# A two-layer graph network on one core: the tensor engine's semaphore increments moved from the last product of a group to a drain behind it

## The reference

```python
def gnn0(x, edge_attr, src, dst):          # 4 heads of 32
    m = x @ W_n2m.T
    q, k, v = m @ Wq.T + bq, m @ Wk.T + bk, m @ Wv.T + bv
    e = edge_attr @ W_edge.T @ We.T        # one row of 128 for each edge
    alpha = sum_c(q[dst] * (k[src] + e)) / sqrt(32)
    alpha = softmax over the edges of one dst
    out = segment_sum((v[src] + e) * alpha, dst)
    x_r = m @ Wskip.T + bskip
    beta = sigmoid([out, x_r, out - x_r] @ Wbeta.T)
    return (beta * x_r + (1 - beta) * out) @ W_m2n.T

def gnn1(x, src, dst, w):                  # one head of 256
    scores = sum(q[dst] * k[src]) / 16 + w * we + be
    attn = softmax over the edges of one dst
    out = segment_sum(v[src] * attn, dst)
    x = layer_norm(x + out + x @ ws + bs)
    return layer_norm(x + gelu(x @ w_ff1 + b1) @ w_ff2 + b2)

x = layernorm(x + gnn0(x, ...)); x = layernorm(x + gnn1(x, ...))
```

## Time and profile before

| | us |
|---|---|
| median of the timed runs | 5051.74 |
| profiled execution, first to last instruction (span) | 6753.4 |
| first node phase | 0 to 107 |
| edge phase of the first layer | 107 to 3131 |
| second node phase | 3131 to 3407 |
| edge phase of the second layer | 3407 to 6401 |
| last node phase | 6401 to 6753.4 |
| TensorE busy / VectorE busy | 4299.6 / 3831.3 |
| ScalarE busy / GpSimd busy | 3003.4 / 3308.1 |
| mean granted TensorE clock | 0.79 |

### The profile page before, as it was taken

One profiled execution on the slowest core, in us unless ns is written; L12 is line 12 of the kernel. 1 busy time (PEld: TensorE's weight loads), 2 busy tenths in 40 slices (PEclk: granted clock), 3 DMA queues, 4 the chain that ended last, 5 costly groups with the idle time before them and its releaser, 6 DMA issues.

```text
span 6753.4 us, 105844 instructions
## 1 busy us (share of the span) xinstructions
PE 4299.6 (64%) x23291; PEld 3492.8 (52%) x23291; DVE 3831.3 (57%) x12902; ACT 3003.4 (44%) x6997; POOL 3308.1 (49%) x3637
## 2 busy tenths in 40 slices
PE   6555555565565566566746666666666666666698
PEld 3454554555455555454534555555554555554587
DVE  4565665666566666666734444455454444444588
ACT  1444454555454454554324444444444444444432
POOL 2545555455555455452355545554555554454355
PEclk8777777777777777777978778787888787777899
DMA  6555555555555555553446556565666665555422
GB/s 201 148 145 148 146 145 146 145 153 148 149 152 145 145 152 154 148 148 99 122 141 163 161 153 162 157 162 157 164 160 158 160 160 158 157 163 158 125 73 70
DMA packets 774181, 996.11 MB, mean 147 GB/s; under 512 B 189569, under 2 KB 559489, under 8 KB 773553
## 3 DMA queue, kind: packets, MB, share of 16 engines
q10 hardware_dynamic: 394272, 443.81, 23.8%
q0 software_dynamic: 150224, 410.39, 22.7%
q1 hardware_dynamic: 229056, 135.14, 7.5%
HBM read 862.98 MB, written 125.90 MB: 146 GB/s over the span
## 4 chain that ended last, share of the span: by engine, by line
another core or an unknown queue 22%; PE 21%; DVE 17%; issue 16%; DVEq 7%; ACTq 5%; ACT 5%; DMA 2%; POOL 2%; SPq 1%; POOLq 1%
PE ps L1377 20%; DVE rows L1009 2%; DVE score L1021 2%; DVE prod L1033 2%; ACT oh L750 2%; DVE acc L1174 2%; DMA acc_d<-acc 2%; ACT place L738 1%; ACTq L827 1%; DVE prod L1016 1%; DVEq L1233 1%; ACTq L730 1%; SPq L266 1%; DVEq L1231 1%
## 5 line engine op out<-in xcount | busy, mean ns | idle before, releaser
L637 POOL DMA_INDIRECT rows<-kv_d,src_all x1564 | 1535.2, 982 | 1543.1 <-DVE score L1021 951.0
L637 POOL DMA_INDIRECT rows<-x_d,src_all x1564 | 1487.0, 951 | 1450.5 <-DVE prod L1033 962.3
L1377 PE MATMUL ps<-place 128*128 128x256 bf16 (+2 forms) x10560 | 1459.9, 288 | 296.4 <-issue 186.8
L1377 PEld LDWEIGHTS ps<-place 128*128 128x128 bf16 (+1 forms) x10560 | 1250.9, 149 | 587.4 <-issue 317.6
L1377 PE MATMUL ps<-rows,oh 128*128 x3520 | 1093.2, 470 | 457.3 <-DVE oh L1154 340.7
L1033 DVE SCALAR_TENSOR_TENSOR prod<-rows,ps 128x256 f32<-128x256 f32 x1760 | 637.3, 418 | 906.8 <-remote 549.9
L1377 PEld LDWEIGHTS ps<-rows,oh 128*128 128x128 f32 x3520 | 797.8, 236 | 617.9 <-issue 478.8
L750 ACT ACTIVATE oh<-iota_row,rel 128x128 f32<-128x128 f32 x2640 | 837.9, 388 | 552.9 <-remote 408.8
L1377 PE MATMUL ps<-msg,oh 128*128 128x132 f32 x3520 | 607.0, 330 | 595.8 <-DVE msg L1149 331.8
L1377 PEld LDWEIGHTS ps<-msg,oh 128*128 128x128 f32 x3520 | 544.1, 235 | 638.9 <-DVE msg L1149 421.0
L738 ACT ACTIVATE place<-dst_row,node_tab 128x512 f32<-128x512 int32 (+1 forms) x880 | 613.2, 708 | 385.4 <-DVE acc L1174 145.3
(11 more groups left out here) (217 smaller groups left out, 4152.9 us busy)
## 6 DMA issues: line engine op xcount, KB each, us to landing
dst_row<-in_dst_row ACTq DMA_DIRECT2D x880, 256.0 KB
place<-q_d ACTq DMA_DIRECT2D x440, 192.8 KB
acc_d<-acc ACTq DMA_DIRECT2D x440, 128.5 KB
ea<-in_ea SPq DMA_DIRECT2D x440, 128.0 KB
acc_d<-acc ACTq DMA_DIRECT2D x440, 66.0 KB
place<-q_d ACTq DMA_DIRECT2D x440, 64.0 KB
rows<-kv_d,src_all POOLq DMA_INDIRECT x1564
rows<-x_d,src_all POOLq DMA_INDIRECT x1564
```

The source lines that it names most:

```text
L637: pool.indirect_dma_start(out=L.rows[:, t % SLOTS, j, 0:D], out_offset=None, in_=L.table, in_offset=bass.IndirectOffsetOnAxis(ap=src_all[: ...
L1377: return pe.matmul(out_, lhsT=lhsT, rhs=rhs, start=first, stop=last)
```

## The change

In both edge phases, each of the ten increments of TensorE moves off the product it stood on: the product has none, and behind it stands `pe.drain()` with the increment. Products, waits, their order, and all other engines are as before. The node phases keep their increments on the products. The drains are 440 each behind edge_keys, queries and back in the first layer, 440 each behind queries (with its bias products) and back in the second, and five for each of 55 chunks in both: 1595 and 1155, in all 2750.

```diff
@@ -1424,8 +1424,8 @@
                         after(pe, s["added"], g - 1)
                         pe.wait_ge(s["ld_ea"][st % PLACES], loads_done(L, c, st))
                         for j in range(JT // 2):
-                            i = mm(e_ps(b)[:, 2 * j * DM:2 * (j + 1) * DM], ea[st % PLACES][:, j * P:(j + 1) * P], w_c[:, :])
-                        i.then_inc(s["e"], 1)
+                            mm(e_ps(b)[:, 2 * j * DM:2 * (j + 1) * DM], ea[st % PLACES][:, j * P:(j + 1) * P], w_c[:, :])
+                        pe.drain().then_inc(s["e"], 1)
 
                 def queries_ready(c, st):
                     pe.wait_ge(s["ld_q"][st % PLACES], loads_done(L, c, st))
@@ -1439,46 +1439,49 @@
                     for j in range(JT):
                         parts = 1 if L is L0 else 3
                         for m in range(parts):
-                            i = mm(q_ps(L, b)[:, j * L.D:(j + 1) * L.D], L.oht[st % PLACES][:, j * P:(j + 1) * P],
+                            mm(q_ps(L, b)[:, j * L.D:(j + 1) * L.D], L.oht[st % PLACES][:, j * P:(j + 1) * P],
                                    L.qw[st % PLACES][:, m * (D + 1):m * (D + 1) + L.D], m == 0, m == parts - 1)
                     if L is L0 or st == 1:
-                        i.then_inc(s["q"], 1)
+                        pe.drain().then_inc(s["q"], 1)
 
                 def bias_products(par, st):
 
                     if L is L1:
                         for j in range(JT):
                             n = st * JT + j
-                            i = mm(qb_ps[par][:, 3 * n:3 * (n + 1)], L.oht[st % PLACES][:, j * P:(j + 1) * P],
+                            mm(qb_ps[par][:, 3 * n:3 * (n + 1)], L.oht[st % PLACES][:, j * P:(j + 1) * P],
                                    L.qw[st % PLACES][:, D::D + 1])
                         if st != 1:
-                            i.then_inc(s["q"], 1)
+                            pe.drain().then_inc(s["q"], 1)
 
                 def turn(c):
                     stand_by(pe, gate, s["masked"], c + 1)
                     sc = biased[:, :, 0:H].rearrange("p n h -> p (n h)") if H == HEADS else biased[:, :, 0]
                     pn = pen[:, :, 0:H].rearrange("p n h -> p (n h)") if H == HEADS else pen[:, :, 0]
                     pe.transpose(turn_ps[0:R, 0:P], sc, ident[:, :])
-                    pe.transpose(turn_ps[0:R, P:2 * P], pn, ident[:, :]).then_inc(s["turned"], 1)
+                    pe.transpose(turn_ps[0:R, P:2 * P], pn, ident[:, :])
+                    pe.drain().then_inc(s["turned"], 1)
 
                 def arrange(c):
                     stand_by(pe, gate, s["ends"], c + 1)
-                    mm(arr_ps[0:H, :], sel_h[H][0:R, :], spread[0:R, :, :].rearrange("p m n -> p (m n)"))\
-                        .then_inc(s["arranged"], 1)
+                    mm(arr_ps[0:H, :], sel_h[H][0:R, :], spread[0:R, :, :].rearrange("p m n -> p (m n)"))
+                    pe.drain().then_inc(s["arranged"], 1)
 
                 def carry_back(c):
                     stand_by(pe, gate, s["carries"], c + 1)
-                    mm(back_ps[0:R, :], sel_ht[H][0:H, 0:R], carry[0:H, :, :].rearrange("p m n -> p (m n)"))\
-                        .then_inc(s["spreadback"], 1)
+                    mm(back_ps[0:R, :], sel_ht[H][0:H, 0:R], carry[0:H, :, :].rearrange("p m n -> p (m n)"))
+                    pe.drain().then_inc(s["spreadback"], 1)
 
                 def turn_back(c):
                     stand_by(pe, gate, s["full"], c + 1)
-                    pe.transpose(turn_ps[:, 2 * P:2 * P + R], full[0:R, :], ident[0:R, 0:R]).then_inc(s["fullT"], 1)
+                    pe.transpose(turn_ps[:, 2 * P:2 * P + R], full[0:R, :], ident[0:R, 0:R])
+                    pe.drain().then_inc(s["fullT"], 1)
 
                 def shrink_first(c):
 
                     stand_by(pe, gate, s["so_in"], c + 1)
-                    mm(so_ps[:, 0:H], first_oh[0:H, :], shrink_d[0:H, 0:H]).then_inc(s["so"], 1)
+                    mm(so_ps[:, 0:H], first_oh[0:H, :], shrink_d[0:H, 0:H])
+                    pe.drain().then_inc(s["so"], 1)
 
                 def back(c, par, st):
                     g, b = CH * c + st, st % 2
@@ -1487,8 +1490,8 @@
                     after(pe, s["acc"], g - 1)
                     summed = msg[st % OHS] if L is L0 else held(x1_rows, slot.pop(g))
                     for j in range(JT):
-                        i = mm(agg_ps(L, b), oh[:, st % OHS, j, :], summed[:, j, :], j == 0, j == JT - 1)
-                    i.then_inc(s["agg"], 1)
+                        mm(agg_ps(L, b), oh[:, st % OHS, j, :], summed[:, j, :], j == 0, j == JT - 1)
+                    pe.drain().then_inc(s["agg"], 1)
 
                 def emit(c, par, scores, sums):
                     past, pp = c - 1, 1 - par
```

## The result

The changed kernel takes 5474.33 us (four runs, 5462.24 to 5484.96), the kernel before 5054.44 us beside it (5045.22 to 5063.39): 1.083 times as long, 95% interval 1.0813 to 1.0847, or 420 us more. The direction was forecast; the size was not: 175 us.

What follows compares the result with a forecast made beforehand. It took the timed kernel to be near GpSimd's gather floor, TensorE and VectorE close behind. (757 + 62) x 0.32 = 262 us, two thirds 175; 5052 + 175 = 5227, forecast 5230, range 5040 to 5480.

Steps and rivals of the forecast that it cites:

- Price of a boundary: TensorE, edge phases: a drain where groups now follow without a gap costs 0.44 us: 0.17 + 0.10 + 0.11 + 0.06.
- Number of seamless boundaries: TensorE, edge phases: 2750 boundaries less 1029 waits leave 1721 without a gap, costing 757 us of TensorE's time.
- How much is on the path: Edge phases: (757 + 62) us times TensorE's chain share 0.32 is 262 us; two thirds of it, 175 us, felt.
- GpSimd's floor: Gathers of the edge phases, 1.25 us each: at least 3998 of 4317 us, swallowing part of the loss; two thirds left.
- mostly an effect of profiling: Increments on products, seen 2.6 us late in the profile, were taken as late mostly because of profiling, not in timed runs.
- The gathers hide it: Rival, edge phases: GpSimd's floor holds and a pair's 4.0 us stay below 4.4, so no change; 5055 us, chance 0.13.
- increments come on time: Rival, waits at L1016, L1033, L1174: increments on drains are not late, so faster; 4900 us, chance 0.17.
- The clock falls: Rival, TensorE in the edge phases: added idle time lowers the granted clock from 0.78 to 0.68; 5400 us, chance 0.20.
- the 1.3 us starts: Sign in the changed profile: edge_keys and queries start 1.3 us behind the group before instead of 0.9, at full clock.
- TensorE's larger share: Sign in the changed profile: the share of TensorE's waits in the chain grows; no size given.
- the longer waits of VectorE: Sign in the changed profile: VectorE waits longer for L1377's products, and GpSimd for scores; no size given.
- the "issue" waits: Sign in the changed profile: TensorE's edge-phase waits grow by some 700 us of short gaps called "issue".

Runs made afterwards that it cites:

- the clean trace: Profile of the kernel before with one idle semaphore instruction in TensorE's queue for each group, increments still on the products; 1.0012 of the kernel before.

## Why the direction was right and the size wrong

**Price of a boundary: right.** 0.44 us forecast, 0.39 to 0.47 measured. For edge_keys into queries its parts are 0.17 of lost overlap (0.17 forecast), 0.23 from the modelled end to the next product, drain and restart together (0.06 + 0.11), and 0.07 for the cold start (1.10 for 1.03; 0.10). The Trainium skill's constant for a lone matmul ("TensorE: Matmul & The Clock Gate", section "Single matmul latency", 163 ns, cited ahead) covers the tail alone, and was a third of it. The Trainium skill's page "PSUM — Partial Sum Buffer", section "Engine vs sequencer instructions", gives its rule, to leave the increment on the producing matmul, as one of correctness; here both ways are correct, and the rule is worth 420 us.

**Number of seamless boundaries: nearly right.** 1721 forecast. The clean trace has 499 waits of TensorE in the first layer's edge phase and 357 in the second's, which leaves 1894.

**"How much is on the path": the step that failed.** The prediction multiplied 819 us of TensorE's time by its share of the chain, 0.32, and again by two thirds for GpSimd's floor, 0.21 in all. The slowdown of 420 us is 0.51 of those 819. So the term that was too small is the part of the added time that is felt: about a half instead of a fifth. Both factors were unfit. The chain's share tells what a *shorter* product would give back to first order; it can't say what a longer one costs once the slack is used up, and in the clean trace, where TensorE has only 14%, it would have missed by more.

What the traces show in its place is a balance. TensorE works its groups in order. In the first layer's edge phase it had 644 us of waits for others and has 242 after, so its queue got longer by 259 (the phase) + 402 (waits that went) = 661 us. Of these the boundaries explain 1096 seamless ones x 0.46 = 504, and the clock, which fell from 0.88 to 0.82, some 100 more: an estimate, from 440 pairs x 2.66 us by the starts of the earlier trace rows = 1170 us, divided by the one and the other. So TensorE's waits took in six tenths of the added time, and the rest is the slowdown.

In the second layer the count is less sure. The waits with a named releaser went from 329 to 283 us. The clean trace has 121 us more of "issue", 83 times, 1.5 us each, which look like waits too. After, 260 us have that name, but in 785 gaps of 0.33 us, mostly the boundaries' own. Without the 121 the waits took in 46 of 170 + 46 = 216 us, a fifth; with them 166 of 336, a half. The clock rose there, from 0.93 to 0.96.

This balance is read after the fact and is no forecast: not all of the 644 us could be filled, since the waits for the scans (L1110, L1092) come back behind every group they follow, however late TensorE is.

**GpSimd's floor: not shown to swallow anything.** In the short condition it waits for scores 255 us before and 653 after, so after the change it follows. Before the change it was close to its floor, in the second layer above all: the clean trace's gathers start from 2572.5 to 4648.5 there, 2076 us against 1955 at 1.25 each. Whether it took in a part of the loss stays open. The factor of two thirds had no row behind it that measured it.

**Late increments "mostly an effect of profiling": wrong.** Every other profiled execution has the time of its own timed run (5483.1 and 5484.96, 7183.6 and 7185.48), and the profile before, 6753.4 us, has that of the timed runs of the long sets (6653 to 6798). So the 1702 us between the profile before and the median came from the two conditions, and the lateness of the earlier trace rows belongs to timed runs of one of them. Putting it down to the profiler led me to take TensorE's share and its waits from a trace of the wrong condition. That the drain waits for the same products and is held by what holds them fits its 9.9 us in the long condition.

**The rivals.** "The gathers hide it" and "increments come on time" are out. Against the first the prediction gave GpSimd's lead as five tiles, 6.3 us; a tile has four gathers, so five tiles are 20 x 1.25 = 25 us, and that argument did not hold. What put the rival out is the result. "The clock falls" was half right: from 0.88 to 0.82 in the first layer, up from 0.93 to 0.96 in the second; the mean of the two phases fell by 0.02, not by 0.10. Of what the profile was to show, there are the 1.3 us starts, TensorE's larger share, the longer waits of VectorE (L1033 for TensorE: 205 us in the clean trace, 339 after) and of GpSimd; the "issue" waits grew by 427 us (126.5 to 553.7), not 700.

## What to carry to other kernels

Keep a semaphore's increment on TensorE's last product: the products' overlap across groups, their weight loads and the queue's running ahead were worth 0.39 to 0.47 us a boundary here, and a drain gives all of it up even where nobody needs its increment. Price added time on an engine that works in order against the waits it has, not by its share of the chain: what its waits for others can't take in is the slowdown. Waits for data that others can make meanwhile shrink; waits for an answer to the engine's own last result stay. And see that profile and median are of one condition before a difference between them is given a cause.

## What the runs showed of the hardware that I had not expected

- Two conditions of a one-core program, 5054 us and 6664 to 6775 us for the same kernel, on one chip in different sets. The long one is longer in the edge phases alone: the node phases of the changed kernel, 253 and 352 us in the short condition, are 254 and 351 in it. Drains of TensorE last up to 9.9 us there against 3.4 (19.9 in the run with two drains), and the granted clock is lower (0.79 against 0.91), as a cause or as an effect; VectorE's and ScalarE's busy times are the same within 1%. What sets the condition was not found.
- A second drain on an empty array takes 13 ns, and 2750 semaphore instructions in TensorE's queue cost 0.1% (0.0 to 0.24).
- A memset and a drain behind GpSimd's gathers stop its queue for 2.6 us.
